# Cross attention: values and row sums in one product per head, the two interleaved halves sorted by masked copies, masked multiply-adds and a lane shuffle

## The reference

```
qp = q @ Wq.T;  k, v = split(latent_kv @ Wkv_expand.T)
scores = einsum('bhqd,bhkd->bhqk', qh, kh) / sqrt(16)
scores = where(causal, scores, min)
attn = softmax(scores)                    # over k
out = einsum('bhqk,bhkd->bhqd', attn, vh) # 16 channels per head
return out @ Wout.T
```

## Time and profile before

| | |
|---|---|
| median of 3 runs | 670.1 us (669.79 to 672.28) |
| the profiled execution | 672.13 us, its span 670.4 us |
| TensorE busy | 93% of the span |
| VectorE / GpSimd / ScalarE busy | 57% / 51% / 40% |
| mean granted clock of TensorE | 0.992 |

### The profile page before, as it was taken

One profiled execution on the slowest core, in us unless ns is written; L12 is line 12 of the kernel. 1 busy time (PEld: TensorE's weight loads), 2 busy tenths in 40 slices (PEclk: granted clock), 3 DMA queues, 4 the chain that ended last, 5 costly groups with the idle time before them and its releaser, 6 DMA issues.

```text
span 670.4 us, 16277 instructions
## 1 busy us (share of the span) xinstructions
PE 620.8 (93%) x6728; PEld 498.1 (74%) x6728; DVE 381.1 (57%) x780; ACT 269.3 (40%) x608; POOL 343.2 (51%) x474
## 2 busy tenths in 40 slices
PE   7987956799999899999999899999999999999996
PEld 6444444445889799755888899854798889899996
DVE  6797778768734454769642544769752444552220
ACT  4957123132335555242335545341325545243332
POOL 7674164214455655614455565615364555508666
PEclk9989989899999999999999999999999999999999
DMA  8911000010121111002031121002021111014220
GB/s 193 361 52 33 1 1 2 1 50 17 40 72 37 41 51 42 11 23 59 26 86 27 37 56 41 21 16 66 22 52 32 37 49 48 22 37 126 65 69 17
DMA packets 41540, 34.15 MB, mean 51 GB/s; under 512 B 9613, under 2 KB 40918, under 8 KB 41466
## 3 DMA queue, kind: packets, MB, share of 16 engines
q1 hardware_dynamic: 39562, 31.27, 17.5%
q10 hardware_dynamic: 1904, 1.84, 0.8%
HBM read 30.92 MB, written 2.17 MB: 49 GB/s over the span
## 4 chain that ended last, share of the span: by engine, by line
PE 45%; DVE 21%; POOL 14%; ACT 8%; issue 8%; DMA 2%; SPq 0%; ACTq 0%; POOLq 0%; DVEq 0%
PE bank L984 7%; DVE A L1451 6%; DVE nm L1528 4%; PE bank L988 4%; PE bank L989 3%; PE bank L990 3%; POOL hb L597 3%; POOL hT_last L685 3%; POOL A L677 3%; PE bank L1161 3%; PE bank L1233 3%; PE bank L1090 3%; ACT A L866 2%; PE bank L1023 2%; PE bank L1079 2%
## 5 line engine op out<-in xcount | busy, mean ns | idle before, releaser
L1426 DVE TENSOR_TENSOR hb<-hb,bank 128x256 f32<-128x256 f32 x102 | 42.7, 419 | 144.5 <-ACT hb L759 144.2
L597 POOL TENSOR_TENSOR hb<-hb,cwb 128x256 f32<-128x256 f32 x102 | 76.2, 747 | 79.6 <-DVE hb L1426 79.5
L587 POOL TENSOR_TENSOR hT<-hb,hT 128x256 fp32r<-128x256 f32 x102 | 79.4, 778 | 73.1 <-ACT hT L749 73.1
L749 ACT ACTIVATE hT<-hb 128x256 fp32r<-128x256 f32 x102 | 42.4, 416 | 122.6 <-POOL hb L597 122.1
L988 PE MATMUL bank<-xTf,wGh 128*128 128x256 f32 x272 | 82.7, 304 | 0.0
L1451 DVE TENSOR_TENSOR A<-bank,decay 128x512 f32<-128x512 f32 x128 | 77.5, 682 | 8.3 <-PE bank L1079 8.1
L989 PE MATMUL bank<-xTf,wUh 128*128 128x256 f32 x272 | 76.8, 282 | 0.0
L989 PE MATMUL bank<-xTf,wGh 128*128 128x256 f32 x272 | 76.8, 282 | 0.0
L990 PE MATMUL bank<-xTf,wGl 128*128 128x256 f32 x272 | 76.6, 282 | 0.0
L988 PE MATMUL bank<-xTf,wUh 128*128 128x256 f32 x272 | 76.6, 281 | 0.0
L990 PE MATMUL bank<-xTf,wUl 128*128 128x256 f32 x272 | 76.5, 281 | 0.0
(11 more groups left out here) (216 smaller groups left out, 1401.7 us busy)
## 6 DMA issues: line engine op xcount, KB each, us to landing
cwb<-cw_rows SPq DMA_DIRECT2D x54, 128.0 KB, 2.9
A<-cw_rows SPq DMA_DIRECT2D x18, 128.0 KB, 3.4
A<-in_x SPq DMA_DIRECT2D x4, 512.0 KB, 4.4
res<-in_x SPq DMA_DIRECT2D x4, 512.0 KB, 4.5
out_x<-res SPq DMA_DIRECT2D x8, 256.0 KB, 2.4
rawG<-in_L_ffn_w_gate SPq DMA_DIRECT2D x2, 704.0 KB, 6.7
rawU<-in_L_ffn_w_up SPq DMA_DIRECT2D x2, 704.0 KB, 7.1
cwb<-cw_rows SPq DMA_DIRECT2D x12, 112.0 KB, 2.8
```

Source lines behind the costliest of these rows:

```text
L587: pool.tensor_tensor(hT[:, c % 2, 1, :], hb[:, c % 2, :], hT[:, c % 2, 0, :].bitcast(F32), ALU.subtract).then_inc(h_lo, 1)
L597: pool.tensor_tensor(hb[:, c % 2, :], hb[:, c % 2, :], cwb[:, c % CWS, :], ALU.mult).then_inc(h_scaled, 1)
L749: act.activation(hT[:, c % 2, 0, :], hb[:, c % 2, :], ACT.Copy).then_inc(h_hi, 1)
L1426: tt(hb[:, c % 2, :], hb[:, c % 2, :], PS[5 + c % 2][:, HT:GT], ALU.mult).then_inc(gu_used, 1)
```

## The change

`onesp` goes. The unused half of each value tile holds ones and no longer zeros, so one product per head gives 16 rows of values and 16 rows of its sum: 16 products per sequence. Head w = 0 goes to columns 0 to 255 of the bank (values in the lower half of each 32-row stripe, sums in the upper), head w = 1 to columns 256 to 511 (the other way round). ScalarE makes two masked copies of the first half, sums and values (`first_heads`; `xcol` holds a 0/1 mask of partitions per half), VectorE adds the second half masked (`second_heads`); that frees the bank (`o_taken`). The sums now stand in the wrong 16 rows: after the reciprocal a `stream_shuffle` swaps the rows of each stripe by halves, then the multiply follows in place in yT. `attended(b)` moves behind the next sequence's ticks a and b. `layer_stats` of the next group moves to b = 0, `layer_apply` is split over b = 1 and 2 and follows the ticks c, and GpSimd's `layer_rstd` moves in front of point x0c. The output projection's first half waits for the first two sequences only.

```diff
-        onesp = sb("onesp", [P, 2, 2 * XD], F32)
+        def sums_of(g, b):
+            return hb[:, 0, :] if g == 0 and b % 2 else rec
+        SWAP = list(range(XD, 2 * XD)) + list(range(XD))
...
-                    pool.memset(xvp...[:, :, w, other], 0.0).then_inc(xvp_zero, 1)
+                    pool.memset(xvp...[:, :, w, other], 1.0).then_inc(xvp_ones, 1)
...
-                    if b == 0 and g == 0:
+                    if b == 0 and g + 1 < NG:
                         layer_rstd(0, g + 1)
                     point(g, f"x{b}c")
-                    if b == 1 and g + 1 < NG and g:
-                        layer_rstd(0, g + 1)
...
+                def first_heads(b):
+                    act.wait_ge(o_part, g * 4 + b + 1)
+                    if g and b:
+                        act.wait_ge(yT_ready, g * 4 + b)
+                    elif g == 0 and b >= 2:
+                        act.wait_ge(yT_ready, b - 1)
+                    src = PS[attend_bank(g, b)][:, 0:2 * P]
+                    act.activation(sums_of(g, b), src, ACT.Copy, scale=xcol[:, 1:2]).then_inc(o_copied, 1)
+                    act.activation(yT[:, :, b * T:(b + 1) * T], src..., ACT.Copy, scale=xcol[:, 0:1]).then_inc(o_copied, 1)
...      (group 0: after point x{b}b, for b = 0 and 2)
+                        first_heads(b)
+                        first_heads(b + 1)
...      (groups 1 to 3: after point x{b}c)
+                        first_heads(b)
...
                 def attend(b):
                     pe.wait_ge(p_ready, g * 16 + 4 * b + 4)
                     if b and g:
-                        pe.wait_ge(yT_ready, g * 4 + b)
+                        pe.wait_ge(o_taken, g * 4 + b)
                     for m in range(2):
-                        for s in range(2):
-                            for w in range(2):
-                                for i in range(4):
-                                    v = xvp[:, b, 8 * m + 2 * i + w, :] if s == 0 else onesp[:, w, :]
-                                    a = (2 * s + m) * T
-                                    last = mm(..., v, weights_of(g, b)..., start=w == 0, stop=w == 1, ...)
+                        for w in range(2):
+                            for i in range(4):
+                                a = (2 * w + m) * T
+                                last = mm(..., xvp[:, b, 8 * m + 2 * i + w, :], weights_of(g, b)..., start=True, stop=True, ...)
...
-                pe.wait_ge(yT_ready, g * 4 + 4)
-                out_projection(yT, [(yT_ready, g * 4 + 4), (yT_ready, g * 4 + 4)], wX[:, 1], (0, 1), wout_ready)
+                if g == 0:
+                    pe.wait_ge(o_taken, 3)
+                out_projection(yT, [(yT_ready, g * 4 + 2), (yT_ready, g * 4 + 2)], wX[:, 1], (0, 1), wout_ready)
+      (inside it, before the second half: pe.wait_ge(yT_ready, g * 4 + 4))
...
+                def second_heads(b):
+                    src, sums, y3 = PS[attend_bank(g, b)][:, 2 * P:4 * P], sums_of(g, b), yT[:, :, b * T:(b + 1) * T]
+                    dve.wait_ge(o_copied, (g * 4 + b) * 2 + 2)
+                    stt(sums, src, xcol[:, 0:1], sums, ALU.mult, ALU.add).then_inc(sums_ready, 1)
+                    stt(y3, src..., xcol[:, 1:2], y3, ALU.mult, ALU.add).then_inc(o_taken, 1)
                 def attended(b):
-                    nc.vector.reciprocal(rec, PS[attend_bank(g, b)][:, 2 * P:4 * P]).then_inc(rec_ready, 1)
-                    tt(yT[...], PS[attend_bank(g, b)][:, 0:2 * P]..., rec..., ALU.mult).then_inc(yT_ready, 1)
+                    nc.vector.reciprocal(sums, sums).then_inc(rec_ready, 1)
+                    nc.vector.stream_shuffle(sums, sums, SWAP).then_inc(rec_swapped, 1)
+                    tt(y3, y3, sums..., ALU.mult).then_inc(yT_ready, 1)
...      (group 0)
+                    second_heads(0)
+                    second_heads(1)
                     attended(0)
-                    attended(1)
                     maxima(2)
                     maxima(3)
                     layer_apply(0, g + 1, tokx, tokx)
+                    attended(1)
                     point(g, "x2a")
+                    second_heads(2)
+                    second_heads(3)
                     attended(2)
                     attended(3)
...      (groups 1 to 3, after points x{b}a and x{b}b)
+                        if b:
+                            attended(b - 1)
+                        elif g + 1 < NG:
+                            layer_stats(0, g + 1, tokx)
                         point(g, f"x{b}c")
+                        if b in (1, 2) and g + 1 < NG:
+                            layer_apply(0, g + 1, tokx, tokx, range(2 * b - 2, 2 * b))
+                        second_heads(b)
+                        if b == GB - 1:
+                            attended(b)
```

More of the change, by code:

```diff
@@ L265, in decoder_layer @@
         o_part = sem("o_part")
+        o_copied = sem("o_copied")
+        sums_ready = sem("sums_ready")
+        o_taken = sem("o_taken")
         rec_ready = sem("rec_ready")
+        rec_swapped = sem("rec_swapped")
         yT_ready = sem("yT_ready")
@@ L515, in _ @@
                                     pattern=[[-1, P]], channel_multiplier=1))
-            made(pool.memset(onesp[:], 0.0))
-            for w in range(2):
-                made(pool.memset(onesp[:, w, XD * w:XD * w + XD], 1.0))
             for n in range(E):
@@ L634, in _ @@
                     other = slice(XD, 2 * XD) if w == 0 else slice(0, XD)
-                    pool.memset(xvp.rearrange("p b (h w) n -> p (b h) w n", w=2)[:, :, w, other], 0.0).then_inc(xvp_zero, 1)
+                    pool.memset(xvp.rearrange("p b (h w) n -> p (b h) w n", w=2)[:, :, w, other], 1.0).then_inc(xvp_ones, 1)
                 if g == 0:
                     pool.wait_ge(w_tp, 9)
-                    pool.wait_ge(xvp_zero, 2)
+                    pool.wait_ge(xvp_ones, 2)
                     for t in (wDh, wDl):
@@ L967, in project @@
                     if n == 0 and g:
-                        pe.wait_ge(yT_ready, g * 4)
+                        pe.wait_ge(o_taken, g * 4)
                     elif n == 3 or n == 4:
@@ L1156, in out_projection @@
                                 pe.wait_ge(*ready[k])
+                            elif done is wout_ready and k == 0:
+                                pe.wait_ge(yT_ready, g * 4 + 4)
                             elif g == 0 and src is gact and k == 0:
@@ L1186, in query_scores @@
                             if i == 0:
-                                pe.wait_ge(yT_ready, g * 4 + b - 1)
+                                pe.wait_ge(o_taken, g * 4 + b - 1)
                         elif g == 0 and b == 1 and i == 0:
@@ L1337, in layer_stats, with layer_apply @@
                     nc.vector.bn_aggr(mv[:, i, b, :], st[:, i, b, :]).then_inc(ln_mean[s], 1)
-            def layer_apply(s, g, src, dst):
+            def layer_apply(s, g, src, dst, batches=range(GB)):
                 i = 0 if s == 0 else 1
                 dve.wait_ge(ln_rstd[s], g + 1)
-                for b in range(GB):
+                for b in batches:
                     ts(dst[:, b, :], src[:, b, :], mv[:, i, b, 0:1], rstd[:, i, b:b + 1], ALU.subtract, ALU.mult).then_inc(xn_ready[s], 1)
```

27 lines of the change are left out of this document (12 added, 15 removed).

## The result

Slower. Four runs of the changed kernel gave a median of 678.02 us (675.64 to 680.02), four of the kernel before beside them 669.94; ratio 1.0095, 95% interval 1.0063 to 1.0128 (the two medians alone give 1.0120, inside it). Forecast were 668.1 us, and a range of 663 to 672.5. The profiled execution took 677.21 us, its span 675.5, against 672.13 and 670.4 before; TensorE's mean granted clock was 0.967 against 0.992.

The account below looks back on a forecast made before the run. VectorE's order was taken to bound the kernel, with TensorE's saving as one of two limits. Gains of 3.5 and 2.0 us less a loss of 3.5 made -2.0: from the median of 670.1 to 668.1 us, range 663 to 672.5.

Parts of the forecast that it names:

- The groups' sum: Whole kernel: group 0 loses 3.5 us, groups 1 and 2 gain 2.0, group 3 gains 3.5; -2.0 us in all.
- VectorE's loop, groups 1 to 3: Cross attention: periods between maxima of 15.85, 17.2 and 16.1 us in groups 1 and 2, with the reciprocal still 1.75.
- Group 3: Last group: VectorE ends 1.6 us earlier and the projection's first half runs ahead; gain 3.5 us.
- The step that failed: Ends of groups 1 and 2: TensorE waits for VectorE, so 1.0 of 3.8 us saved remains per group.
- the -2.0 of groups 1 and 2: Groups 1 and 2: a gain of 1.0 us each, from shorter loops less a loss behind the fourth maxima.
- Group 0, forecast 3.5: First group: no ticks hide VectorE's added work; last multiply at 121.3 instead of 117.45 us, loss 3.5 us.
- A: Rival: TensorE's saving lands, group 0 loses 1.5 us, groups 1 to 3 gain 3.5 each; 661.1 us, chance 0.20.
- B: Rival: VectorE's reciprocal from SBUF and GpSimd's tick scaling block each other, 15 us in all; 683 us, chance 0.08.
- C: Rival: the shuffle in `attended` is slow, at the reciprocal's 1.75 us adding 9.1 us; 677 us, chance 0.10.

Follow-up runs that it names:

- fill12: The changed kernel plus idle products (results never read) in two of TensorE's waits in groups 1 and 2; 674.0 us, ratio 1.0062 to the kernel before.
- after: The changed kernel with no further edit, against the kernel before; median 678.02 us, ratio 1.0095.
- old0fill: The changed kernel with group 0 in the form of before, plus idle products in groups 1 and 2; 666.14 us, ratio 0.9939 to the kernel before.
- fill0: The changed kernel plus idle products in TensorE's waits of groups 0, 1 and 2; 671.46 us, ratio 1.0006 to the kernel before.
- keep: The changed kernel plus idle products in some of TensorE's waits in group 0; 675.54 us, ratio 1.0052 to the kernel before.
- swapfill: The changed kernel, idle products in groups 0 to 2, and group 0's attended(0), attended(2) ahead of second_heads(1), second_heads(3); 669.69 us, ratio 0.9969 to the kernel before.
- old0fill0: The changed kernel with group 0 in the form of before, plus idle products in groups 0, 1 and 2; 664.64 us, ratio 0.9918 to the kernel before.

## Why the prediction was wrong

The groups' sum was forecast at -2.0 us and came to +4.6 in the traces. Of these 6.6 us groups 1 and 2 are 3.4, group 0 is 2.6, group 3 is 0.6.

**VectorE's loop, groups 1 to 3: right.** Its periods stand within about 0.2 us, the reciprocal from SBUF at PSUM's pace included. Without clock falls a group takes 152.9 (fill12) instead of 153.5 to 154.0: 0.6 to 1.0, forecast 1.0. Group 3: 2.9, forecast 3.5.

**The step that failed** is the one that read: "TensorE arrives at 278.98 with its turning over 2 us early and waits for VectorE: of the 3.8 us of products saved in the group, 1.0 remain." It took the saved 2.8 us for free idle time. They are not: the pause is followed, in 12 of 20 cases, by 3 to 4 us of products at 1.2 GHz that stand on the path, 1.5 us each time. With 12 in five executions hit that is 3.6 us on the mean; the idle products gave back 2.2 us in fill12 (ratio 1.0062 for 1.0095) and 2.3 in old0fill (0.9939 for 0.9974), plus or minus 2 to 3 by the intervals, and in the profiled spans of after and fill12 4.0, of which two falls are 3.1. That alone turns the -2.0 of groups 1 and 2 into a small loss. The clock had been read as a mean of 0.992 and never as something that the change could move.

**Group 0, forecast 3.5, measured 6.1.** Two terms of the sum were too small. Of the 3.0 us by which the last multiply came later than forecast, 0.5 lie ahead of the third maxima and 1.87 are the wait for `attend(3)`, for which the sum "then `attended(1)` 2.6, split 1.6, `second_heads` 0.7 twice, `attended` 2.6 and 2.7: 121.3" has no term: key products and both attends at half clock take 0.91 + 0.85 + 0.86 us more. Most of the rest is the split of the weights beside GpSimd's masking, 2.15 instead of 1.71. fill0 took the wait away and met GpSimd's own split: 3.44 us instead of 2.15, so only 1.0 us of the group came back. So the clock alone is not group 0's loss; the larger part of it, 3.5 us for VectorE's added work, was in the forecast. The group costs more than the first trace says: its old form took 117.0 to 117.2 in three later traces, not 118.53, and against these the loss is 7.4 us. What the forecast's order of VectorE would bring with neither of the two is not shown by any run.

**The rivals.** A (the saving lands) is refuted: TensorE's waits at the groups' ends are there. B (VectorE and GpSimd block each other) holds as a mechanism in another place than it was put: not at the reciprocal, where it was to decide, but at the multiply, harmless, and at the split of the weights in group 0. C falls with a shuffle of 0.43 to 0.46. The Trainium skill ("VectorE: DVE Perf Modes", section on the perf-mode tier table) gives a shuffle the one-element-per-cycle tier alone, the same as a multiply of f32; the trace agrees, with 0.42 for the multiply of this width. The way in which it really went, slower by TensorE's clock, was not among the rivals.

**Open.** Why the clock falls behind a pause of 1.9 us in one execution and not in the next is shown by no run, nor is what decides the fall at 86 us. That the old form of group 0 gained 1.4 to 1.5 us from idle products (117.0 to 117.2 in three traces without, 115.67 with; 119.99 in a fourth, old0fill, where the clock fell further) rests on one trace; that filling the pause ahead of the tail's turning shortens the tail rests on three (80.63, 80.85 and 80.98 in keep, swapfill and old0fill0; 81.80 to 83.50 in the ten others).

## What to carry to other kernels

Work taken from TensorE where another engine sets the pace becomes a pause, and the pause has a price: look at what TensorE does right behind it, at the granted clock of that stretch, and in several traces rather than one, since it comes and goes. Before a saving is counted, ask which engine each end of a stretch hangs on; a few idle products in the wait tell whether the clock is the cost. And where two loops are of nearly one length, apply such a change group by group: here it pays in the last, does little in the two in the middle, and costs in the first, where nothing hides VectorE's new work.

## What was not expected of the hardware

A wait of 1.90 to 1.97 us on TensorE, after 30 us and more with none above 0.9, was followed by a fall of the granted clock from 1.00 to 0.50 for 3 to 4 us in 12 of 20 cases; with 7 or 8 idle products in it and 0.2 to 0.4 us left open, in 0 of 20 (five kernels). With the products of group 0's `attend` issued twice the clock fell there all the same. Two splits of weights beside each other, VectorE's two of 128x768 and GpSimd's two of 128x512, took 3.44 and 3.39 us, where they took 1.28 and 2.51 on their own.
